# A two-layer transformer kernel: moved step places in attention, the gated state added in half precision, earlier base rows, and the row gathers in four pairs

## The chip, the cores and the metric

One core of one Trainium2 chip runs the whole program. Times are device microseconds; the time before is the median of three runs, and one further execution was taken with the hardware profiler. The engines are PE (TensorE), DVE (VectorE), ACT (ScalarE), POOL (GpSimd) and SP (SyncE, which issues DMAs).

## The reference

Two layers over x of 8 x 512 tokens, 256 wide. Each layer adds two branches of the normalised input to x.

```
xn = layernorm(x)
x  = x + attention0(xn) + moe0(xn)
xn = layernorm(x)
x  = x + gated_scan1(xn) + moe1(xn)

attention0:  16 causal heads of 16, softmax, output projection
moe0:        shared expert + 2 of 8 routed experts, silu((xW1+b1)*(xW3+b3)) W2 + b2, H = 352
gated_scan1: z = sigmoid(xWz+bz); h_t = (1-z_t) h_{t-1} + z_t (xWh+bh)_t; sigmoid(hWg+bg) * h
moe1:        latent 128, 2 of 8 experts (all computed, weighted), relu^2; shared relu^2(x up) down
```

## The kernel before, in words

**Precision.** Most products of full-precision operands are made of three half-precision products (`three_products`, lines 121 to 123): each operand is split into a high half, a half-precision copy made by ACT, and a low half, the difference, made by DVE or POOL.

**Three phases.** `mix_phase` is attention with the router of the first layer. `experts_phase` runs the first layer's experts over tiles of 256 tokens: 11 of the 16 shared tiles (head), then the routed tiles of eight experts in a hardware loop, then the last 5 shared tiles (the tail), in which the second layer's first block of 512 tokens is already prepared. `layer1_phase` runs eight steps, one for each block; step 0 and step 7 are written out, the six between are a hardware loop of two steps a turn. It has the longest code on each engine, and every engine runs its own list of instructions in order; semaphores with names such as `sc_s` (router sigmoid done) join the lists.

**Attention's order is written out by hand.** A block has 16 heads and a head three units, so a block has 48 places. At each place PE makes one unit of a head's scores transposed (`scores_k`, L854 to L858) and one unit of the next but one group's scores (`scores_q`, L839), whose row maxima DVE takes (`maxima`, L687) out of two banks in turn: PE may be two units ahead. Groups are four heads. DVE turns a group's maxima (L695) at its last place, and ACT issues four small DMAs (`load_max`, L486) that put them into the query stack, one at each of the places 0 to 3 of the group; `scores_k` of the next group waits for them. Everything else has a place of its own, given by the `AT_` constants: the next block's transposed input, q, k, v and logits; the previous block's transposed output and projection; the router; and for the block after next the statistics, the normalised rows (`normalise`, L566, two tiles at each of places 25 and 26) and `x_bias` on POOL. An operation that PE makes at a place is copied by ACT one place later, and its low half or sum is made by DVE two places later. The q and k halves are stored by SP and fetched again into the stacks (`load_stacks`, L308 to L325); the first half of the heads is needed by `scores_q` at place 24, the second at place 0 of the next block.

**The second layer's step.** PE makes the router's logits, the latent, z0, h0 (waits for `sc_s`), z1 (waits for the latent's low half), h1, eight `up` parts, the gate of the scanned state, eight experts with the `down` products between them, the next block's transposes, `combine`, then the sixteen adds of the gated state to the output banks (L2318) and the latent's last product (waits for `comb_lo_s`). ACT begins with the sigmoid L1970, then the latent's high half, the sigmoids of z, relus (L1955), squares and high halves. DVE does the router, the two injections, the scans (L2111), `sums` (L2037), low halves and the experts' squares. POOL does, in this order, the eight row gathers of the next block (`gather`, L1887: 128 rows of 1 KB each, from `y_routed`), `base` (L1894: x1 plus the shared experts' y, after `total_y` of the block before has read the buffer), four `up_low` and eight `he_lo`. The gathers wait only for the slots and for the last `sums`, so they start as soon as POOL has done the last `he_lo` of the step before. `sums(b + 1, k)` adds the weighted rows k of the next block to its base, first k = 0, later k = 1. The gated state is `gh = gs * hT` in full precision, and PE adds it by a matmul against the identity:

```
for t in range(TT):
    for c in range(DC):
        pe.matmul(out_bank[t][:, c * P:(c + 1) * P], gh[:, c, t * P:(t + 1) * P], identf[:, :],
                  start=False, stop=False)
```

**The base rows of block 0.** SP loads `xin` and `ysh` (x1 and y of the first 512 tokens) in `new_expert(E + 1)`, behind the last routed tile's store. POOL then adds them (L1325), waits for that store and issues eight gathers (L1331); DVE adds the rows in the tail's tiles 2 and 3 (`first_sums`).

## Time and profile before

| what | value |
|---|---|
| median of 3 runs | 1267.59 us (1266.76 to 1270.79) |
| the profiled execution's own time | 1274.47 us |
| its span | 1272.7 us |
| PE busy | 1134.8 us (89%) |
| DVE busy | 914.3 us (72%) |
| ACT busy | 677.0 us (53%) |
| POOL busy | 550.2 us (43%) |

Attention lasts to about 480 us of the span, the experts to 857, the second layer to the end. A step of the second layer takes 52 us and an attention block 53 to 57. A busy time is the union of an engine's instructions; a matmul's end is modelled, so PE's rows overlap, and a PE is idle only where a row has a bracket. A bracket at a row's end gives the idle time of that engine before it and what ended it; "remote" is a releaser that the trace does not name, "issue" is no wait that it shows.

### The profile page before, as it was taken

How to read it: one execution, taken by the hardware profiler on the slowest of the kernel's cores; microseconds unless marked ns; L12 is line 12 of the kernel's file. 1: busy time of each engine (PE TensorE's matmuls, PEld its weight loads, DVE VectorE, ACT ScalarE, POOL GpSimd, SP SyncE). 2: the span in 40 equal slices, each digit the busy share in tenths (PEclk: the TensorE clock that was granted, in tenths of full speed). 3: DMA queues.
4: the chain of work that ended last, by engine and by line, in shares of the span. 5: the costliest groups of instructions: out<-in, count | busy, mean ns of one | idle time of the engine just before them, and what ended most of it. 6: DMA issues, size and time to landing. Idle time of an engine off the chain costs nothing. (4 is left out here: it accounts for less than half of the span.)

```text
span 1272.7 us, 26804 instructions
## 1 busy us (share of the span) xinstructions
PE 1134.8 (89%) x8933; PEld 764.3 (60%) x8965; DVE 914.3 (72%) x2208; ACT 677.0 (53%) x1462; POOL 550.2 (43%) x758
## 2 busy tenths in 40 slices
PE   4888998888989885999999999969888998998998
PEld 2344554455455544998999898944554645545555
DVE  5678797778878835986666776748595685965965
ACT  2256565555555544666656766635364353652553
POOL 5432333323233226934444444224554735546324
PEclk9689999999999997999999999979999999999999
DMA  4337524335433204545422544424131331323203
GB/s 136 73 83 200 102 43 92 76 71 100 65 76 59 44 18 148 173 131 164 121 85 82 156 123 153 130 65 164 34 117 51 126 124 33 116 84 99 83 1 100
DMA packets 96846, 124.07 MB, mean 97 GB/s; under 512 B 14192, under 2 KB 86448, under 8 KB 95728
## 3 DMA queue, kind: packets, MB, share of 16 engines
q1 hardware_dynamic: 85744, 103.89, 30.5%
q0 software_dynamic: 6912, 18.88, 5.3%
q8 instruction: 47, 0.77, 0.3%
q10 hardware_dynamic: 4096, 0.14, 0.2%
q14 instruction: 47, 0.39, 0.1%
HBM read 83.52 MB, written 39.19 MB: 96 GB/s over the span
## 5 line engine op out<-in xcount | busy, mean ns | idle before, releaser
L476 ACT ACTIVATE p<-bank 128x384 f32<-128x384 f32 (+1 forms) x384 | 193.0, 528 | 196.1 <-PE bank L854 152.8
L687 DVE TENSOR_REDUCE neg_max<-bank 128x1 f16<-128x384 f32 (+3 forms) x352 | 218.8, 641 | 81.9 <-PE bank L842 72.5
L396 POOL TENSOR_SCALAR_AFFINE_SELECT p<-p 128x256 f32<-128x256 f32 x256 | 103.7, 410 | 260.9 <-ACT p L476 259.9
L121 PE MATMUL xbank<-gT_hi,w_hi 128*128 128x256 f16 (+1 forms) x636 | 175.6, 276 | 15.6 <-DVE gT_lo L1444 7.8
L122 PE MATMUL xbank<-gT_lo,w_hi 128*128 128x256 f16 (+1 forms) x636 | 175.5, 276 | 0.0
L123 PE MATMUL xbank<-gT_hi,w_lo 128*128 128x256 f16 (+1 forms) x636 | 175.4, 276 | 0.0
L839 PE MATMUL bank<-k_stack,q_stack 96*128 96x384 f16 (+3 forms) x512 | 134.5, 315 | 38.3 <-DVE neg_max L687 29.0
L1366 ACT ACTIVATE a<-xbank,b 128x256 f32<-128x256 f32 x159 | 74.4, 469 | 63.3 <-PE xbank L123 62.4
L1275 POOL DMA_INDIRECT fetched<-xn_dram,token_now x80 | 82.1, 1027 | 42.9 <-POOL token_now L1271 30.7
L854 PE MATMUL bank<-q_stack,k_stack 97*128 97x512 f16 (+1 forms) x256 | 91.8, 363 | 5.8 <-ACT p L476 3.3
L1451 DVE SCALAR_TENSOR_TENSOR prod<-xbank,b,a 128x256 f32<-128x256 f32 x159 | 74.0, 476 | 30.5 <-ACT a L1366 25.6
L1920 POOL TENSOR_TENSOR he_lo<-he_sq,he_hi 128x512 f16<-128x512 f32 x64 | 75.8, 1203 | 41.6 <-ACT he_hi L2006 41.6
L839 PEld LDWEIGHTS bank<-k_stack,q_stack 96*128 96x128 f16 x512 | 47.0, 100 | 77.5 <-DVE neg_max L687 54.9
L121 PE MATMUL ybank<-l_xT_hi,pack_hi 128*128 128x512 f16 x208 | 80.8, 389 | 13.1 <-ACT l_sc L1970 4.0
L121 PE MATMUL xbank<-w_hi,h_hi 128*128 128x256 f16 (+1 forms) x318 | 87.6, 275 | 1.9 <-DVE y L1466 1.9
L123 PE MATMUL xbank<-w_hi,h_lo 128*128 128x256 f16 (+1 forms) x318 | 87.5, 275 | 0.4 <-issue 0.4
L122 PE MATMUL xbank<-w_lo,h_hi 128*128 128x256 f16 (+1 forms) x318 | 87.5, 275 | 0.0
L2006 ACT ACTIVATE he_hi<-he_sq 128x512 f16<-128x512 f32 x64 | 39.4, 627 | 85.4 <-DVE he_sq L2139 85.4
L1457 DVE TENSOR_TENSOR h_lo<-h,h_hi 128x256 f16<-128x256 f32 x159 | 67.7, 429 | 22.0 <-ACT h_hi L1375 17.9
L121 PEld LDWEIGHTS xbank<-gT_hi,w_hi 128*128 128x128 f16 (+1 forms) x636 | 68.3, 107 | 24.8 <-issue 15.3
L122 PE MATMUL ybank<-l_xT_lo,pack_hi 128*128 128x512 f16 x208 | 80.6, 387 | 2.7 <-issue 2.7
L872 PE MATMUL bank<-p,v_aug 128*32 128x512 f32 (+3 forms) x1024 | 82.0, 438 | 0.8 <-DVE o_rows L667 0.8
(300 smaller groups left out, 3043.9 us busy)
## 6 DMA issues: line engine op xcount, KB each, us to landing
w_bc<-wT_dram SPq DMA_DIRECT2D x8, 2048.0 KB, 8.3
y_routed_dram<-y SPq DMA_DIRECT2D x37, 256.0 KB
w<-in_w SPq DMA_DIRECT2D x11, 704.0 KB
pack<-in_pack SPq DMA_DIRECT2D x12, 342.0 KB
xr<-in_x SPq DMA_DIRECT2D x8, 512.0 KB, 7.3
xn_dram<-xn SPq DMA_DIRECT2D x8, 512.0 KB, 3.7
qk_hi_dram<-qk_hi SPq DMA_DIRECT2D x16, 256.0 KB, 2.2
qk_lo_dram<-qk_lo SPq DMA_DIRECT2D x16, 256.0 KB, 2.2
```

The source lines that it names most:

```text
L121: pe.matmul(out, hi_a(c), hi_b(c), start=first and x == 0, stop=False)
L122: pe.matmul(out, hi_a(c), lo_b(c), start=False, stop=False)
L123: mm = pe.matmul(out, lo_a(c), hi_b(c), start=False, stop=last and x == n - 1)
L396: pool.affine_select(out=diagonal, in_=diagonal, pattern=[[0, 2], [1, P]], compare_op=ALU.is_ge, fill=0.0, base=0, channel_multiplier=-1). ...
L476: act.activation(p32[:, s // GH % 2, s % GH, cols], s_bank[n][:, 0:cols.stop - cols.start], ACT.Exp).then_inc(p_exp.sem, 1)
L687: dve.tensor_reduce(neg_max[:, g % 2, 0:GH * TT].rearrange("p (h t) -> p h t", t=TT)[:, heads[0]:heads[-1] + 1, j], a_bank[c % 2][:, 0:len ...
L839: pe.matmul(to[:, at * w:(at + 1) * w], q_stack[0:STK, u, h0 + h, j * P:(j + 1) * P], k_stack[0:STK, u, h0 + h, 0:w], start=at == 0, stop= ...
L854: mm = pe.matmul(to[:, 0:S - n * P], k_stack[0:AUG, u, h, n * P:(n + 1) * P], q_stack[0:AUG, u, h, n * P:S], start=True, stop=True)
L872: mm = pe.matmul(out_bank[VW * h:VW * (h + 1), k * P:S], v_aug[:, b % 2, k, GH * (g % NG) + h, :], p32[:, g % 2, h, P_OFF[k]:P_OFF[k] + S ...
L1275: pool.indirect_dma_start(fetched[:, u, half, :], None, dram["xn"], bass.IndirectOffsetOnAxis(token_now[:, u, half:half + 1], 0)).then_inc ...
L1366: act.activation(a1[0:M, m, :], bank[m][0:M, 0:ETOK], ACT.Identity, bias=b13[0:M, u, m:m + 1]).then_inc(a1_s.sem, 1)
L1920: pool.tensor_tensor(he_lo[:, e, :], he_sq[:, e % EB, :], he_hi[:, e, :], ALU.subtract).then_inc(he_lo_s.sem, 1)
```

## The change

Places: the transposed input goes from 0 and 2 to 1 and 3, the first q from 6 to 7, the transposed output from 13 and 16 to 14 and 17, the second projection from 24 to 25, the second v from 36 to 37; the normalised rows go from two tiles at 25 and 26 to one at each of 28 to 31, `x_bias` from 28 to 33, the router's ranks from 14 to 19 to six places up to 24; the maxima's four DMAs go out two at a place. The loads of block 0's base rows move from behind the routed tiles to the end of the head tiles. In the second layer the gathers are cut into four pairs, k = 0 first, each behind a step of ACT, with a semaphore for each k. The gated state is formed in place in `gs`, split by ACT and DVE into halves, and added by PE with a half-precision identity.

```diff
-AT_X_T, AT_Q, AT_K, AT_OUT_T, AT_PROJ, AT_V, AT_LOGITS = (0, 2), (6, 27), (9, 30), (13, 16), (21, 24), (33, 36), 39
-AT_STATS, AT_RSTD, AT_NORM, AT_XB = (21, 22), 24, (25, 26), 28
-AT_SCORES, AT_CHOICE, AT_WEIGHTS, AT_RANK_SUMS, AT_RANKS = (4, 6), (7, 8), 10, 12, (14, 15, 16, 17, 18, 19)
-AT_MAX = (0, 1, 2, 3)
+AT_X_T, AT_Q, AT_K, AT_OUT_T, AT_PROJ, AT_V, AT_LOGITS = (1, 3), (7, 27), (9, 30), (14, 17), (21, 25), (33, 37), 39
+AT_STATS, AT_RSTD, AT_NORM, AT_XB = (21, 22), 24, (28, 29, 30, 31), 33
+AT_SCORES, AT_CHOICE, AT_WEIGHTS, AT_RANK_SUMS, AT_RANKS = (4, 6), (7, 8), 10, 12, (15, 16, 18, 19, 20, 24)
+AT_MAX = {0: (0, 1), 1: (2, 3)}
...
-                        q = AT_MAX.index(at % (U * GH))
-                        load_max(group(s) - 1, range(q, q + 1))
+                        load_max(group(s) - 1, AT_MAX[at % (U * GH)])
...
-                            normalise(b + 2, halves[AT_NORM.index(at)])
+                            normalise(b + 2, range(AT_NORM.index(at), AT_NORM.index(at) + 1))
...
                 if is_int(e, E + 1):
-                    sp.wait_ge(y_stored.sem, y_stored.at(HEAD_TILES - 1))
-                    sp.dma_start(front.xin[:, :, :], token_rows(dram["x1"])).then_inc(front.xin_loaded.sem, 16)
-                    sp.dma_start(front.ysh[:, :, :], token_rows(dram["y"])).then_inc(front.xin_loaded.sem, 16)
                     return
...
             def last(e, u, first):
                 if is_int(e, 0):
                     store(HEAD_TILES - 1, dram["y"], HEAD_TILES - 1)
+                    sp.wait_ge(y_stored.sem, y_stored.at(HEAD_TILES - 1))
+                    sp.dma_start(front.xin[:, :, :], token_rows(dram["x1"])).then_inc(front.xin_loaded.sem, 16)
+                    sp.dma_start(front.ysh[:, :, :], token_rows(dram["y"])).then_inc(front.xin_loaded.sem, 16)
...
-                elif stage == 2:
+                elif stage == TAIL_TILES - 3:
                     first_sums(0)
                     first_sums(1)
-                elif stage == 3:
+                elif stage == TAIL_TILES - 2:
...
-        gathered = sig("rows_gathered", 16 * TT * 2)
+        gathered = [sig(f"rows_gathered{k}", 16 * TT) for k in range(2)]
...
-            def gather(b):
+            def gather(b, k, tiles):
...
-                for t in range(TT):
-                    for k in range(2):
-                        pool.indirect_dma_start(rows_k[:, t, k, :], None, dram["y_routed"],
-                                                bass.IndirectOffsetOnAxis(slot[:, t, k:k + 1], 0)).then_inc(gathered.sem, 16)
+                for t in tiles:
+                    pool.indirect_dma_start(rows_k[:, t, k, :], None, dram["y_routed"],
+                                            bass.IndirectOffsetOnAxis(slot[:, t, k:k + 1], 0)).then_inc(gathered[k].sem, 16)
...
             def step(b, u, before, more):
                 if more:
-                    gather(b + 1)
+                    pool.wait_ge(sc_s.sem, sc_s.at(b))
+                    gather(b + 1, 0, (0, 1))
+                    pool.wait_ge(zs_s.sem, zs_s.at(b, 1))
+                    gather(b + 1, 0, (2, 3))
+                    pool.wait_ge(zs_s.sem, zs_s.at(b))
+                    gather(b + 1, 1, (0, 1))
+                    pool.wait_ge(r_s.sem, r_s.at(b, 2))
+                    gather(b + 1, 1, (2, 3))
                     base(b + 1, 1 - u)
...
                 for c in range(DC):
                     act.wait_ge(g_psum.sem, g_psum.at(b, c + 1))
+                    act.wait_ge(gh_lo_s.sem, gh_lo_s.at(b - 1, c + 1))
...
                 if more:
                     x_high(b + 1)
+                for c in range(DC):
+                    act.wait_ge(gh_s.sem, gh_s.at(b, c + 1))
+                    act.wait_ge(out_psum.sem, out_psum.at(b - 1))
+                    act.activation(gh_hi[:, c, :], gs[:, c, :], ACT.Copy).then_inc(gh_hi_s.sem, 1)
...
-                dve.wait_ge(gathered.sem, gathered.at(b - 1, 0))
+                for k in range(2):
+                    dve.wait_ge(gathered[k].sem, gathered[k].at(b - 1, 0))
...
-                    dve.tensor_tensor(gh[:, c, :], gs[:, c, :], hT[:, c, :], ALU.mult).then_inc(gh_s.sem, 1)
+                    dve.tensor_tensor(gs[:, c, :], gs[:, c, :], hT[:, c, :], ALU.mult).then_inc(gh_s.sem, 1)
                 if more:
                     x_low(b + 1)
+                for c in range(DC):
+                    dve.wait_ge(gh_hi_s.sem, gh_hi_s.at(b, c + 1))
+                    dve.tensor_tensor(gh_lo[:, c, :], gs[:, c, :], gh_hi[:, c, :], ALU.subtract).then_inc(gh_lo_s.sem, 1)
...
-                pe.wait_ge(gh_s.sem, gh_s.at(b))
+                pe.wait_ge(gh_lo_s.sem, gh_lo_s.at(b))
                 for t in range(TT):
                     for c in range(DC):
-                        pe.matmul(out_bank[t][:, c * P:(c + 1) * P], gh[:, c, t * P:(t + 1) * P], identf[:, :],
-                                  start=False, stop=False)
+                        for gh in (gh_hi, gh_lo):
+                            pe.matmul(out_bank[t][:, c * P:(c + 1) * P], gh[:, c, t * P:(t + 1) * P], front.identh[:, :],
+                                      start=False, stop=False)
```

## Rows read from the trace of the kernel before

**Rows 1.** The page's first line

```profile
span 1272.7 us, 26804 instructions
```

**Rows 2.** Stretches: span, busy PE, PEld, DVE, ACT, POOL; granted clock, DMA share, GB/s

```profile
97.00:150.00 53.00, 47.40 (x423) 27.51 (x426) 42.91 (x113) 30.31 (x63) 18.48 (x37) 1.00 0.62 159
...
600.00:700.00 100.00, 99.58 (x912) 91.45 (x910) 66.29 (x151) 63.48 (x168) 44.28 (x62) 1.00 0.32 95
```

**Rows 3.** Waits: who waited for whom, us in total, times, longest

```profile
ACT l_sc L1970 <- remote: 47.5, 6, 7.9
```

**Rows 4.** Timeline of POOL, second layer: start, length, instruction, idle before

```profile
1017.70 0.95 POOL L1887 DMA_INDIRECT rows_k<-y_routed_dram,slot  x1 [0.30 <-issue]
...
1028.83 2.36 POOL L1894 TENSOR_TENSOR x<-xin,ysh 128x1024 f32<-128x1024 f32 x1 [10.18 <-DVE l_y L2146]
```

**Rows 5.** Timeline of ACT, the same step and, from 1223, the last

```profile
1020.40 0.20 ACT L1970 ACTIVATE l_sc<-ybank 128x32 f32<-128x32 f32 x1 [7.89 <-remote]
...
1027.18 0.60 ACT L1955 ACTIVATE r<-ybank 128x512 f32<-128x512 f32 x1 [1.41 <-PE ybank L123]
1028.39 0.60 ACT L1955 ACTIVATE r<-ybank 128x512 f32<-128x512 f32 x1 [0.61 <-PE ybank L123]
...
1223.92 0.20 ACT L1970 ACTIVATE l_sc<-ybank 128x32 f32<-128x32 f32 x1 [3.08 <-PE ybank L123]
...
1231.71 0.60 ACT L1955 ACTIVATE r<-ybank 128x512 f32<-128x512 f32 x1 [1.32 <-PE ybank L123]
```

**Rows 6.** Timelines of POOL and ACT, end of the expert stage

```profile
822.38 2.36 POOL L1325 TENSOR_TENSOR x<-xin,ysh 128x1024 f32<-128x1024 f32 x1 [20.66 <-DMA ysh<-y_dram]
...
833.75 0.95 POOL L1331 DMA_INDIRECT rows_k<-y_routed_dram,slot  x1 [0.30 <-issue]
...
836.46 0.60 ACT L1358 ACTIVATE gT_hi<-xbank 128x512 f16<-128x512 f32 x1 [5.34 <-remote]
```

**Rows 7.** Timeline of DVE, the step of rows 4

```profile
1029.63 2.65 DVE L2111 TENSOR_TENSOR_SCAN hT<-keep,inject 128x512 f32<-128x512 f32 x1
...
1032.78 1.21 DVE L2111 TENSOR_TENSOR_SCAN hT<-keep,inject 128x512 f32<-128x512 f32 x1
...
1033.91 1.64 DVE L2037 SCALAR_TENSOR_TENSOR x<-rows_k,wk,x 128x256 f32<-128x256 f32 x4
```

**Rows 8.** Timelines of PE and DVE, end of a second-layer step

```profile
1063.95 1.95 PE L2318 MATMUL ybank<-identf,gh 128*128 128x128 f32 x16
1065.73 0.27 PE L121 MATMUL ybank<-pack_hi,comb_hi 128*128 128x256 f16 x1
...
1064.78 0.69 DVE L2191 TENSOR_TENSOR comb_lo<-ybank,comb_hi 128x512 f16<-128x512 f32 x1 [4.15 <-ACT comb_hi L2012]
```

**Rows 9.** Groups of instructions, the table matmuls: busy us, mean ns, idle before

```profile
L1670 PE MATMUL xbank<-in_column,in_lane 128*128 128x114 f16 x64 | 3.5, 213 | 0.0
```

**Rows 10.** Timeline of PE in attention: places 5, 24, 29, 41 and 45 of block 1

```profile
110.83 0.34 PE L839 MATMUL bank<-k_stack,q_stack 96*128 96x384 f16 x1 [1.04 <-DVE neg_max L687]
...
131.90 0.39 PE L839 MATMUL bank<-k_stack,q_stack 96*128 96x128 f16 x4
...
139.12 0.34 PE L839 MATMUL bank<-k_stack,q_stack 96*128 96x384 f16 x1 [1.41 <-DVE neg_max L687]
...
153.06 0.34 PE L839 MATMUL bank<-k_stack,q_stack 96*128 96x384 f16 x1 [0.87 <-DVE neg_max L687]
...
157.81 0.39 PE L854 MATMUL bank<-q_stack,k_stack 97*128 97x512 f16 x1 [0.29 <-DMA q_stack<-max_rows]
```

**Rows 11.** Timeline of DVE, places 25 and 26 of the same block

```profile
135.32 0.81 DVE L566 TENSOR_SCALAR xn<-xr,mv,rstd 128x256 f32<-128x256 f32 x2
...
137.87 0.72 DVE L566 TENSOR_SCALAR xn<-xr,mv,rstd 128x256 f32<-128x256 f32 x2
```

**Rows 12.** Timeline of SP's queue, the store of k's low half

```profile
120.85 0.36 SPq L308 DMA_DIRECT2D qk_lo_dram<-qk_lo  x1
```

**Rows 13.** Groups of instructions, the routed tiles' gathers

```profile
L1275 POOL DMA_INDIRECT fetched<-xn_dram,token_now x80 | 82.1, 1027 | 42.9 <-POOL token_now L1271 30.7 <-issue 12.2
```

More of the change, by code:

```diff
@@ L1025, in __init__ @@
         self.xT_hi, self.xT_lo = (sb(f"l1_xT_{k}", [P, DC, S], F16) for k in ("hi", "lo"))
+        self.identh = sb("identh", [P, P], F16)
+        self.identh_s = sig("identh_s", 1)
         self.tile_out = sb("y", [P, ETOK // P, D])
@@ L1078, in experts_phase @@
         tail_at = sb("tail_at", [P, TAIL_PLACES])
-        identh = sb("identh", [P, P], F16)
+        identh = front.identh
         pos_part = sb("pos_part", [P, 2, T // P, 2], I32)
@@ L1118, in experts_phase @@
         lane_placed = sig("lane_placed", 1)
-        identh_s = sig("identh_s", 1)
+        identh_s = front.identh_s
         lanes_half_s = sig("lanes_half_s", 1)
@@ L1729, in layer1_phase @@
         gs = sb("gs", [P, DC, S])
-        gh = sb("gh", [P, DC, S])
+        gh_hi, gh_lo = (sb(f"gh_{k}", [P, DC, S], F16) for k in ("hi", "lo"))
         lat_hi, lat_lo = (sb(f"lat_{k}", [P, S], F16) for k in ("hi", "lo"))
@@ L1804, in layer1_phase @@
         gh_s = sig("gh_s", DC)
+        gh_hi_s = sig("gh_hi_s", DC)
+        gh_lo_s = sig("gh_lo_s", DC)
         out_psum = sig("out_psum", TT)
@@ L2032, in sums @@
                     dve.wait_ge(x2_base.sem, x2_base.at(b))
-                    dve.wait_ge(gathered.sem, gathered.at(b - 1))
+                    dve.wait_ge(gathered[0].sem, gathered[0].at(b - 1))
                 else:
+                    dve.wait_ge(gathered[1].sem, gathered[1].at(b - 1))
                     dve.wait_ge(x2_sum.sem, x2_sum.at(b, 1))
```

## The prediction

> **What bounds the kernel now.** I read the page's first line for the span, then the long waits, then the busy time by stretch, and then the timelines of the three places that the change touches. The profiled execution took 1274.5 us around a span of 1272.7 us [rows 1]. The median of the timed runs is 1267.6 us, so the profile is 6.9 us heavy. I make the sum against 1274.5 and carry it to the median by taking the same 6.9 us off. A measurement of this kernel tells about 0.3% (3.8 us) from no change.
>
> The reader should see three regimes in [rows 2]: attention (PE busy 47.40 of 53 us), the routed tiles (99.58 of 100, nothing to gain there), and the second layer, whose steps are 52 us apart. PE sets the pace of attention except where it waits, so its idle rows are the gain on offer. In the second layer one wait stands out: ACT waits before the router's sigmoid (L1970) six times, 47.5 us in all, for a releaser the profile cannot name [rows 3].
>
> **Second layer, the gathers (the largest term).** In the step before 1020.40, the last of POOL's eight back-to-back row gathers is issued at 1017.70 and done at 1018.65 [rows 4]; ACT's sigmoid starts at 1020.40, 1.75 us after that, after 7.89 us idle [rows 5]. At the end of the expert stage the same eight gathers end at 833.75 + 0.95 = 834.70, and ACT's copy that waits for PE starts at 836.46, 1.76 us after it, again "remote" [rows 6]. Two places, one distance: while a long run of gathers is under way, PE's releases reach the others late, and the last ones when the last gather has landed. The last step issues no gathers and shows the wait without them: 3.08 us [rows 5]. So a step loses 7.89 - 3.08 = 4.81 us. The change makes POOL wait for that very sigmoid before its first gather, so the hold can't fall there any more.
>
> Part comes back. During the hold PE runs ahead into the latent and z0 products; without it the first relu comes 1231.71 - 1223.92 = 7.79 us after the sigmoid in place of 1027.18 - 1020.40 = 6.78: 1.01 us back. The second piece is `base`, the add of 2.36 us on POOL (1028.83, [rows 4]), which now stands behind the fourth pair. That pair waits for the second relu. Measured from the sigmoid, this relu ends about 9.6 us on (28.39 + 0.60 - 20.40 = 8.6 in the old step, plus 1.01). Two gathers take 1.25 + 0.95 = 2.2 us (spacing and length of [rows 4]), so base runs from about 11.9 to 14.3. Before, it ran from 8.43 to 10.79, and the first scan that met it took 2.65 us where the second took 1.21 [rows 7]: DVE's scan stood still until POOL's add was over. Now the second scan meets it: it started at 1032.78, 12.38 on, and could start at 12.38 + 1.01 = 13.4, waits to 14.3 and ends at 15.4, where `sums` started at 1033.91, 13.51 on, before. From `sums` on DVE is without a pause until the experts are done, so the whole tail shifts by 1.9 us, in which the 1.01 is contained. Net per step 4.81 - 1.9 = 2.9; six steps: **17.4 us**. From below: if base costs nothing, 3.8 x 6 = 23. From above: see the second rival. Step 0 had its gathers after the products anyway; I count nothing.
>
> The Trainium skill (SBUF — State Buffer, "SBUF: two separate sides") says that a DVE operation with two SBUF inputs and a GpSimd operation that reads SBUF exclude each other for the whole instruction. The trace agrees: 2.65 against 1.21 us. It speaks against this change, because it sets base against a later scan, and without the lock the step would gain 3.8 instead of 2.9.
>
> The rest of POOL's queue behind the gathers: base, then the four up_lows, which wait for ACT's up_hi of square 4, late in the step, and keep their cover. sums(k=1) needs the fourth pair's rows only at 19.7 us after the sigmoid, the pair is issued by 12. The split of the gathered semaphore costs DVE one more wait that has long been met.
>
> **The gated state in half precision.** PE's sixteen full-precision adds take 1.78 us to the next matmul (1063.95, the next row's start being 1065.73, [rows 8]). Thirty-two half-precision ones of the same 128 columns: 64 table matmuls of 114 columns took 3.5 us, 55 ns each [rows 9], so 32 x 55 = 1.76 us. And both lie inside the wait for comb_lo, written from 1064.78 to 1065.47: even at half the price PE would go on no sooner than 1065.5. Taken: 0, bounds -0.3 and +0.5 us a step. ACT's two added copies (0.6 us each as its other copies) and DVE's two subtractions (0.69 us as comb_lo) fall between the transposed input and comb_hi, where ACT is idle for 4.4 us and DVE for 4.2. Cost 0; without that cover 1.3 us a step.
>
> **Base rows sooner.** POOL waited 20.66 us for xin and ysh, added them from 822.38 to 824.74 and then gathered [rows 6]. Now both tiles are there early, and the first gather waits only for the last routed store, which SP issues right before those two loads: some 5 us sooner, an estimate from what the loads' landing took. The 1 MB moves beside the first routed tiles, where DMA engines are a third busy (0.32, [rows 2]). But the hold (ACT idle 5.34 us before 836.46 in the same rows) moves with the gathers to the tile before, at the same price. What can go is DVE's waits for rows, which PE doesn't feel. Taken: 0.5 us; bounds -2 and +3. The two stage numbers written as TAIL_TILES minus something are the same numbers as before.
>
> **Attention places.** A place (a third of a head) is 1.1 us of PE. Take the block from 105.5 to 158.9 [rows 10]. At place 5 PE waits 1.04 us for DVE's maximum: DVE had the divide, one x_low and then another with the scores. The change moves x_low from places 2 and 4 to 3 and 5. Of 1.04 I take 0.9. At place 29 it waits 1.41 us, because DVE ran divide, residual and four normalised tiles through places 25 and 26 (the tiles alone 0.81 and 0.72, [rows 11]). The change puts the residual at 27 and a tile each at 28 to 31. I take 1.2. At place 41 it waits 0.87 (v_bias, now at 39), and at place 45 0.29 for the maxima's DMA, now issued two places sooner. But those rows queue beside the stacks' loads, and a PE that is early there only waits longer: I take 0.4 of 1.16. Between places 12 and 24 I take nothing: PE starts on the next block's stacks at 131.90 without a wait, and their arrival is set by a chain of DMAs that begins when k's low half is stored, after place 11 (120.85, [rows 12]): store, its landing, six loads of 128 KB. Whatever PE saves before place 24 it waits there. Sum 2.5 us a block, six full blocks, 1 us for the first and last: **16 us**. Bounds: 0.5 a block (the new places only move the waits: the transposed output's low half is now a place later, with the projection at 21 waiting for it) and 4 a block. The moved x_bias on POOL (2.4 us, place 28 to 33) delays no mask that a value product waits for; its DVE neighbours change, its length doesn't.
>
> **Sum.** 17.4 + 0 + 0.5 + 16 = 33.9: 1274.5 becomes 1240.6 profiled, 1267.6 becomes 1233.7; I say 1234.
>
> **The rivals.**
> *Only the gathers help* (0.12): the attention waits move to the stacks' and maxima's DMAs. For it: no wait at 131.90. Against it: places 29 and 5 are plain DVE backlog. 1267.6 - 17.9 = 1250, within 1.
> *The hold follows the gathers* (0.15): each run of gathers delays PE's releases wherever it stands, and now it stands where ACT, DVE and PE hand over every 1.3 us. Against it: the routed stage issues 80 gathers two at a time [rows 13] and its PE is 99.6% busy. For it: three of the four pairs follow nearly at once. If 2.5 of the 2.9 us go, 1267.6 - 16.5 - 2.4 = 1249.
> *Neither helps* (0.05): 1265.
> *Slower* (0.06): each pair holds releases until its own landing, 2.2 + 1.75 = 3.95 us, and three of the four pairs have someone waiting: 11.9 us held plus 1.9 for base against 4.81 saved is +9.0 a step, +54 in all, less 16.5: 1305. It decides against the change as soon as the holds pass about 5.6 us a step (2.9 + 16.5 / 6).
> *The forecast* (0.62).
>
> The range runs from 1217 (3.8 a step, 4 a block) to 1256 (half of either term and a dearer base). Faster by more than 0.3%: 0.89; within: 0.05; slower: 0.06.
>
> **What would show it.** ACT's idle before L1970 near 3 us and never "remote"; steps 49 us apart in place of 52; base starting 12 us after the sigmoid with a long second scan; PE's wait for neg_max below half; the wait at place 24 put down to the k_stack load; L2318 with 256 matmuls and no wait for gh_lo. It is wrong if "remote" waits appear before the relus or zs, or if attention's span stays within 3 us of before.

## The result: 0.992 of the time before, a quarter of the forecast gain

The changed kernel takes 1259.73 us (median of seven runs, 1254.64 to 1265.4) against 1268.36 (1266.76 to 1271.89) for the kernel before, a ratio of 0.9921 with a 95% interval of 0.9904 to 0.9939. The forecast was 1234, with a range from 1217 to 1256. The gain is 8.6 us where 33.6 were expected.

The profiled execution of the changed kernel took 1258.37 us, about its median. That of the kernel before took 1274.47, heavier than all seven of its timed runs, so the two profiles differ by 16.1 us, of which 6.1 are the older profile's excess over its median and 1.4 are what the newer one lies below its own.

Of the page, kernel after, the first line and the group of the second layer's gathers (busy us, mean ns, idle before and what ended most of it); POOL now stands 63.3 us waiting for the sigmoid, which is what the change asks of it:

```profile
span 1256.6 us, 26994 instructions
...
L1889 POOL DMA_INDIRECT rows_k<-y_routed_dram,slot x56 | 61.9, 1105 | 91.9 <-ACT l_sc L1979 63.3
```

Where the 16.1 us are is read from two landmarks that both kernels have: the copy of the identity at the start of the expert stage, and the eight router sigmoids of the second layer. The tile view of each kernel (first the kernel before, then the one after: count, durations in ns, first and last start):

```profile
L1413 ACT ACTIVATE identh<-identf x1: 309/309/309, 481.9 to 481.9; 128x128 f16<-128x128 f32 x1
...
L1970 ACT ACTIVATE l_sc<-ybank x8: 197/198/198, 862.1 to 1223.9; 128x32 f32<-128x32 f32 x8
```

```profile
L1414 ACT ACTIVATE identh<-identf x1: 309/309/309, 463.2 to 463.2; 128x128 f16<-128x128 f32 x1
...
L1979 ACT ACTIVATE l_sc<-ybank x8: 197/197/198, 845.0 to 1208.1; 128x32 f32<-128x32 f32 x8
...
  PE ybank L123: 20.2, 7
```

Attention ends 18.7 us sooner. The experts take 381.8 us in place of 380.2. The seven steps between the first and the last sigmoid take 363.1 us in place of 361.8: **the second layer, where 17.4 us were expected, gives nothing**. And yet the wait of [rows 3] is gone: seven sigmoids now idle 20.2 us together, 2.9 each, and none is put down to "remote". The hold went, and something of the same size came.

The timeline of DVE, POOL and ACT in one step (its sigmoid at 1055.31; four of the seven steps are like it) shows what, beside [rows 4, 5, 7]:

```profile
1055.31 0.20 ACT L1979 ACTIVATE l_sc<-ybank 128x32 f32<-128x32 f32 x1 [2.89 <-PE ybank L123]
...
1065.63 1.21 DVE L2127 TENSOR_TENSOR_SCAN hT<-keep,inject 128x512 f32<-128x512 f32 x1
...
1065.78 1.81 POOL L1889 DMA_INDIRECT rows_k<-y_routed_dram,slot  x1 [1.59 <-issue]
...
1067.90 0.95 POOL L1889 DMA_INDIRECT rows_k<-y_routed_dram,slot  x1 [0.30 <-issue]
...
1068.22 4.10 DVE L2127 TENSOR_TENSOR_SCAN hT<-keep,inject 128x512 f32<-128x512 f32 x1
...
1068.87 2.35 POOL L1896 TENSOR_TENSOR x<-xin,ysh 128x1024 f32<-128x1024 f32 x1
...
1072.24 1.64 DVE L2053 SCALAR_TENSOR_TENSOR x<-rows_k,wk,x 128x256 f32<-128x256 f32 x4
```

The first gather of the fourth pair meets the first scan and takes 1.81 us where the next takes 0.95. The second scan begins while the last gather is under way and ends at 1072.3, 1.1 us after POOL's add is over: it stood through the gather and the add that follows it without a pause. The sums start 16.93 us after the sigmoid; in the step of [rows 5, 7] it was 13.51.

The other three steps (sigmoids at 845.01, 898.00 and 1001.64) lose the time in another way. No scan is long in them: both gathers of the fourth pair meet a scan, the add starts 14.1 to 15.1 us after the sigmoid, and the sums wait for it until 16.6 to 17.6. Timelines of POOL and DVE in the step from 1001.64:

```profile
1015.04 1.70 POOL L1889 DMA_INDIRECT rows_k<-y_routed_dram,slot  x1 [0.30 <-issue]
...
1016.76 2.36 POOL L1896 TENSOR_TENSOR x<-xin,ysh 128x1024 f32<-128x1024 f32 x1
...
1019.25 2.57 DVE L2053 SCALAR_TENSOR_TENSOR x<-rows_k,wk,x 128x256 f32<-128x256 f32 x4 [3.26 <-POOL x L1896]
```

PE, which waits for the scanned state's high half, shows the price twice. The timeline of PE, step from 1055.31:

```profile
1072.18 0.38 PE L123 MATMUL ybank<-l_xT_hi,pack_lo 128*128 128x512 f16 x1
1075.75 0.39 PE L121 MATMUL ybank<-hT_hi,pack_hi 128*128 128x512 f16 x1 [3.19 <-DVE up_sq L2132]
...
1077.62 0.63 PE L122 MATMUL ybank<-hT_lo,pack_hi 128*128 128x512 f16 x1
1078.05 0.63 PE L123 MATMUL ybank<-hT_hi,pack_lo 128*128 128x512 f16 x1
```

It idles 3.19 us, and then the matmuls, 0.21 us apart before, are 0.43 us apart: the granted clock has fallen to half, 1.2 GHz. A stretch of this step and one of the step from 1001.64, in which PE idled 4.71 us, until 1023.68 (columns as in [rows 2]; the rest of both steps has 1.00):

```profile
1076.90:1080.30 3.40, 3.40 (x10) 1.22 (x9) 3.40 (x4) 1.64 (x4) 3.40 (x3) 0.50 0.88 295
```

```profile
1022.30:1029.10 6.80, 5.42 (x13) 1.94 (x14) 5.67 (x11) 2.35 (x4) 2.56 (x2) 0.50 0.97 309
```

3.4 us at half clock cost 1.7 us. Four of the seven steps have 3.4 us of it, two (from 845.01 and 1001.64) have 6.8, the last has none: 27.3 us in all, of which PE was idle for 2.3, so 12.5 us are lost, where the kernel before loses 1.7. Over the seven the granted clock is 0.96, where it was 0.99 before. The first row is before, the second after:

```profile
862.10:1223.90 361.80, 327.97 (x2076) 189.26 (x2076) 265.93 (x598) 172.76 (x322) 183.65 (x171) 0.99 0.27 89
```

```profile
845.00:1208.10 363.10, 325.37 (x2076) 187.97 (x2076) 272.87 (x612) 182.71 (x336) 197.25 (x175) 0.96 0.28 88
```

In attention PE's wait for the row maxima falls from 27.2 to 10.1 us (waits of PE from 51 to 480 us, before and after):

```profile
PE bank L839 <- DVE neg_max L687: 27.2, 42, 1.5
```

```profile
PE bank L838 <- DVE neg_max L686: 10.1, 29, 1.4
```

### The profile page after: what moved, and what is told of

It is laid out like the page before. It is cut to its first block and busy times, and to the rows that moved or that the text cites. A ratio compares the mean times of both kernels' runs of the same rounds, so it can differ in the third digit from the quotient of the medians.

```text
span 1256.6 us, 26994 instructions
## 1 busy us (share of the span) xinstructions
PE 1133.0 (90%) x8964; PEld 756.0 (60%) x8965; DVE 921.3 (73%) x2224; ACT 683.9 (54%) x1478; POOL 559.2 (45%) x758
## 5 line engine op out<-in xcount | busy, mean ns | idle before, releaser
L1889 POOL DMA_INDIRECT rows_k<-y_routed_dram,slot x56 | 61.9, 1105 | 91.9 <-ACT l_sc L1979 63.3
L1929 POOL TENSOR_TENSOR he_lo<-he_sq,he_hi 128x512 f16<-128x512 f32 x64 | 77.1, 1223 | 32.2 <-ACT he_hi L2016 32.2
L841 PE MATMUL bank<-mask_qk,identb 128*128 128x128 bf16 (+2 forms) x352 | 88.6, 252 | 0.0
```

Of the source, the lines that this page charges most:

```text
L841: pe.matmul(diagonal, identb[:, :], mask_qk[:, 0:len(heads), :], start=False, stop=True).then_inc(a_psum.sem, 1)
L1929: pool.tensor_tensor(he_lo[:, e, :], he_sq[:, e % EB, :], he_hi[:, e, :], ALU.subtract).then_inc(he_lo_s.sem, 1)
```

## The experiments

Sixteen runs stand in four groups, each group on one chip with its own runs of the kernel before: 1270.27, 1245.72, 1245.05 and 1271.15 us. I call the first and the last chip A and D, the others B and C. Between groups only ratios and the lengths of stages are compared.

**Which stage, which part (chip A).** One: the kernel before again, unchanged.

> The kernel before, unchanged, profiled once more, because its profiled execution (1274.47 us) lies above all seven of its timed runs (1266.76 to 1271.89). If the two profiles differ by a stage, the router's sigmoids of the second layer or the start of the expert stage stand elsewhere than at 862.06 to 1223.92 and 481.92 us. Theory 1 (the excess is chance, spread over the stages): attention ends within 2 us of 482, the seven intervals between sigmoids sum to 362 within 2 us. Theory 2 (the change's gain in attention is partly an unlucky execution of before): attention ends 4 to 7 us sooner here. In both the held sigmoids are there: six waits of 7.9 us.

1269.86 us. Attention ends at 477.5 in place of 481.9, the seven steps take 361.7 us (857.7 to 1219.4), and the sigmoids are held as before:

```profile
L1413 ACT ACTIVATE identh<-identf x1: 309/309/309, 477.5 to 477.5; 128x128 f16<-128x128 f32 x1
...
L1970 ACT ACTIVATE l_sc<-ybank x8: 197/197/198, 857.7 to 1219.4; 128x32 f32<-128x32 f32 x8
...
  remote: 47.7, 6
```

So theory 2: of the 4.6 us between the two profiled executions 4.4 lie in attention. Against this execution attention's gain is 14.3 us, not 18.7. It is one execution, and whether its chip is that of the first profile isn't known.

Two: the places alone (`AT_` constants, `load_max`, `normalise`; the rest as before).

> Before, with the new places of attention alone. Theory 1 (the profile's 18.7 us between the two kernels in attention are this part's): 1268 - 17 = 1251, within 3, and the second layer as before with six held sigmoids near 7.9 us. Theory 2 (only part of it is real, the rest chance of one execution): 1256 to 1260.

1257.04 us, 0.9883 (0.9856 to 0.9910): 13.2 us less. Attention ends at 463.2 as in the changed kernel, the second layer is the old one (361.5 us, six held sigmoids, 47.5 us). The stage saves the 14 that the second profile of before says: theory 2.

Three: all but the places.

> The changed kernel with the places of attention as before; gathers in pairs, half-precision gated state and the sooner base rows stay. Theory 1 (in the second layer what the sigmoid no longer waits, the second scan waits behind POOL's last pair and its add of the base rows): 1268 within 3, the intervals between sigmoids 51 to 52 us, the second scan about 4.1 us long. Forecast of the record: 1250. Theory 2 (a loss that the attention places hide): above 1272.

1280.05 us, 1.0066 (1.0043 to 1.0090): **the other three parts together make the kernel slower by 9.8 us**, where the forecast had 17.9 faster. The steps take 373.7 us, 52.4 to 54.3 each, and neither theory names the cause. It isn't the scan that stands still here (none takes over 1.22 us) but POOL: both gathers of the fourth pair meet a scan (1.81 and 1.70 us), the add starts only 15.2 us after the sigmoid, and the sums wait for it until 17.7 (the step from 959.6; the others are alike). PE then waits 4.6 to 4.8 us, and 6.8 us are at half clock in five of the seven steps, 3.4 in two, 41 us in all. The code has the pair wait for the second relu of ACT, and that relu was released late, after the third pair of gathers (timeline of ACT; at this place it idles 0.70 us in the changed kernel's step from 1055.31, and 1.3 to 1.7 in that kernel's three steps without a long scan):

```profile
969.49 0.60 ACT L1965 ACTIVATE r<-ybank 128x512 f32<-128x512 f32 x1 [1.54 <-PE ybank L123]
```

Four: the add moved.

```diff
                     gather(b + 1, 0, (2, 3))
+                    base(b + 1, 1 - u)
                     pool.wait_ge(zs_s.sem, zs_s.at(b))
                     gather(b + 1, 1, (0, 1))
                     pool.wait_ge(r_s.sem, r_s.at(b, 2))
                     gather(b + 1, 1, (2, 3))
-                    base(b + 1, 1 - u)
```

> The changed kernel with POOL's add of the base rows (2.35 us) moved ahead of the third pair of gathers, so that it lies from about 6.3 to 8.7 us after the sigmoid, between the two scans' inputs and the first scan at 10.3. Theory 1 (the second scan waits for the base add, which POOL begins in the same moment as the last gather lets go): the second scan falls from 4.1 us to 1.2 or 1.9, the sums start near 14.3 us after the sigmoid in place of 16.9, seven steps each lose 2.6: 1260 - 18 = 1242, within 4. Theory 2 (PE's releases are held behind each pair of gathers, wherever the add is): the step stays at 51 us and the time at 1260, within 3.

1250.01 us, 0.9831 (0.9806 to 0.9857): 20.3 us less than before, between the two theories. The second scan takes 1.21 us and the first sums start 14.04 us after the sigmoid, as theory 1 has it. But the add waits for DVE's `total_y` until 8.66 us after the sigmoid, so the last gathers are late, and the second sums wait 5.13 us for their rows; PE then waits 2.61 and again runs 3.4 us at half clock (timelines of POOL, DVE and PE in the step from 995.7, then a stretch):

```profile
1012.15 1.28 POOL L1889 DMA_INDIRECT rows_k<-y_routed_dram,slot  x1 [0.30 <-issue]
...
1021.12 1.67 DVE L2053 SCALAR_TENSOR_TENSOR x<-rows_k,wk,x 128x256 f32<-128x256 f32 x4 [5.13 <-DMA rows_k<-y_routed_dram,slot]
...
1024.65 0.39 PE L121 MATMUL ybank<-lat_hi,pack_hi 128*128 128x512 f16 x1 [2.61 <-DVE he_sq L2155]
```

```profile
1025.00:1028.40 3.40, 3.40 (x16) 2.01 (x14) 3.30 (x8) 1.47 (x3) 2.31 (x2) 0.50 0.02 5
```

Step 0, where the last gather was done at 14.0 and no sum waited, took 48.0 us, the others 51.

Why those rows are late can be read from the trace, though no run tested it. The last gather starts at 1012.15, and at 1012.65 SP issues the load of `w_bc`, 2 MB, and by 1014.42 three more of 512 KB. The DMA engines are then nearly full until the rows are there, where in the 4 us before their busy share was 0.29 (timeline of SP, then a stretch):

```profile
1012.65 0.35 SPq L1871 DMA_DIRECT2D w_bc<-wT_dram  x1
```

```profile
1012.70:1020.70 8.00, 7.70 (x49) 4.47 (x48) 3.15 (x5) 5.04 (x10) 5.84 (x5) 1.00 0.92 299
```

In step 0 the last gather was done 2.5 us before this load was issued, and its rows came in time.

**The next order, and the small parts (chip B).** Five: the add between the third and the fourth pair.

```diff
                     gather(b + 1, 1, (0, 1))
+                    base(b + 1, 1 - u)
                     pool.wait_ge(r_s.sem, r_s.at(b, 2))
                     gather(b + 1, 1, (2, 3))
-                    base(b + 1, 1 - u)
```

> The changed kernel with POOL's add of the base rows between the third and the fourth pair of gathers. In the kernel that has it before the third pair, the second scan is cured but the last gather is done only at 17.7 us after the sigmoid, its rows arrive at 24.95 and the second sums start at 25.4 in place of 20.4, whereas its step 0, with the last gather done at 14.0, needs 47.96 us. Theory 1 (a step is 48 us when neither a scan nor the second sums wait): pair three stays at 6.7 to 8.9, the add runs from 8.9 to 11.3 with the first scan behind it (done near 12.4 in place of 11.5), pair four is done near 13.5, the second sums start by 21: six to seven steps of 48 to 48.5 us, the granted clock near 1.00 in them, 1260 - 7 x 3 = 1239, within 4. Theory 2 (the gathers hold PE's releases wherever they are, so a step with eight of them can't be under 51 us): 1256 to 1262.

1228.01 us, 0.9865 (0.9843 to 0.9888). The steps are 47.2 to 49.1 us, and no clock is lost in them: theory 1 for the steps. But the ratio is no better than attention's alone, because this chip's kernel before takes 1245.72, and the next three say why.

Six: one run of eight gathers behind the sigmoid, then the add.

> The changed kernel with the eight gathers in one run directly behind the sigmoid, without ACT's steps between the pairs, then the add of the base rows. Theory 1 (a long run of gathers holds PE's releases until its end, as before the sigmoid in the kernel before): the run goes from 1.1 to 11.1 us, the latent's copy, the zs and the relus late by 4 to 5 us, the step 53 us or more, 1270 or above. Theory 2 (nothing is held: the idle time before the sigmoid had another cause; only the exclusion with DVE's scans costs): the run ends at 11.1, the add at 13.5, the first scan waits a gather, the second about 1.2 us, and the step is under 50: 1248 or less.

1235.33 us, 0.9911 (0.9887 to 0.9935), steps of 48.4 to 49.8. The relus start 7.8 to 7.9 us after the sigmoid (6.55 in step 0), in the middle of the run, as with no gathers: nothing is held here, theory 2 on this chip.

Seven and eight: one small part each.

> The kernel before with the half-precision gated state alone. The record said 0, between -0.3 and +0.5 us a step, because both forms end inside PE's wait for comb_lo; if the cover were missing it would be 1.3 us a step. Theory 1: 1270, within 3 us, PE's wait before the combine's products longer by what the products save. Theory 2 (the shorter products do come through, since the copies on ACT and the subtractions on DVE take the time between the input's low half and comb_hi): 1262 to 1266. Theory 3 (the added operations push comb_hi and so the next sigmoid): 1275 or more.

> The kernel before with the two loads of the first base rows issued one expert sooner, nothing else. The record said 0.5 us less, between -2 and +3 saved. Theory 1: 1270, within 3 us; POOL's wait for the rows shorter by 5 us or more, ACT's hold in the last routed tiles at another tile but as long. Theory 2 (the hold goes with the run of gathers into a tile where PE has slack): up to 5 us less, 1265.

1244.23 us, 0.9985 (0.9971 to 1.0000), and 1245.21 us, 1.0000 (0.9981 to 1.0019): theory 1 of both, with 1.5 us, if anything, for the first. Both have the gathers of the kernel before, in one run that passes over the sigmoid, and no sigmoid is held (tile view of the eighth kernel, then its seven steps as a stretch):

```profile
L1970 ACT ACTIVATE l_sc<-ybank x8: 197/198/198, 854.5 to 1193.3; 128x32 f32<-128x32 f32 x8
...
  PE ybank L123: 21.6, 7
```

```profile
854.50:1193.30 338.80, 321.29 (x2075) 189.74 (x2076) 264.02 (x598) 173.94 (x323) 182.59 (x172) 1.00 0.30 95
```

**The hold on which the largest term rested comes and goes with the chip.** These steps take 361.7 us on chip A and 338.8 here with the same code of the second layer: 22.9 us, where the medians of the kernel before are 24.6 apart. The experts are 4.8 us shorter here as well, attention 1.6 longer. Each chip was used in one group of runs only, so a property of the chip and a state that it was in can't be told apart.

**All on one chip without a hold (chip C).** Nine to twelve: the changed kernel, the gathers alone, everything but the gathers, and the fifth kernel again.

> The changed kernel unchanged, beside the three that follow, on one chip. So far one chip gave 1270 us for the kernel before, with the held sigmoids in its profile, and another 1246, where the same order of gathers has steps of 48 to 49 us and no held sigmoid. Theory 1 (the hold is a property of the chip, and the pair order costs what it costs on either): on the chip of 1270 it is 0.992 of before as recorded; on the chip of 1246 the second layer gets slower than before by 2 to 3 us a step (the scan behind the add), and only attention's 14 us stand against it: 1246 - 14 + 7 x 2.6 = 1250, a ratio of 1.00. Theory 2 (the hold goes with the kernel, not with the chip): a ratio of 0.992 on both.

> The kernel before with the gathers in four pairs and the add behind them alone. Theory 1: on the chip of 1270, 1280 as with the half-precision state and the sooner base rows beside it (1.007); on the chip of 1246, no hold to remove, so the full price of the late add shows: 1246 + 18 = 1264, a ratio near 1.015. The record's term (17.4 us less) would be 0.986. Theory 2 (the price came from the half-precision state's added waits beside the gathers): 1.00 or less.

> The changed kernel with the gathers and the add as before. Theory 1: attention's gain alone, and nothing from the other two: 0.988 of before on either chip, and on the chip of 1246 the fastest of the four or level with the next. Theory 2 (the parts need each other): over 0.995.

> The changed kernel with the add between the third and the fourth pair, once more, to stand beside the other three on one chip. Theory 1: on the chip of 1246 again 0.9865, level with the kernel that has the gathers as before, since there is no hold there to gain from; on the chip of 1270 steps of 48 to 49 us in place of 51 to 52, so 1240 or a ratio of 0.977. Theory 2 (on the chip of 1270 the gathers late in the step arrive late, as the fourth pair did at 24.95 us after the sigmoid): 51 us a step, 0.985.

| kernel | median us | ratio (95%) | seven steps, us |
|---|---|---|---|
| the kernel before | 1245.05 | | |
| changed kernel | 1241.92 | 0.9972 (0.9956 to 0.9988) | 353.3 |
| gathers alone | 1259.53 | 1.0104 (1.0080 to 1.0128) | 357.3 |
| all but the gathers | 1225.78 | 0.9847 (0.9825 to 0.9869) | 337.3 |
| add before the last pair | 1229.05 | 0.9867 (0.9846 to 0.9888) | 339.6 |

Theory 1 is the nearer one throughout, though three of its numbers were too high: the changed kernel came to 1242 where it had 1250, the gathers alone to 1259.5 for 1264, all but the gathers to 0.985 for 0.988. That last kernel saves 19.3 us here, where the places alone saved 13.2 on chip A and the two small parts 1.5 and 0 on chip B; no run shows where the other 4 to 5 us come from. Where nothing is held the four pairs with the add behind them cost 14.5 us alone, 16 in the changed kernel (1241.92 against 1225.78). Two of its seven steps have the long scan that four had in the first profile. In the other five the second scan starts at the same place and takes 1.21 us, and it is the add that is long: it takes 2.7 us in place of 2.35, and the sums wait 2.3 us for it (a step of each kind: scan, then add):

```profile
1002.46 1.22 DVE L2127 TENSOR_TENSOR_SCAN hT<-keep,inject 128x512 f32<-128x512 f32 x1
...
1003.12 2.72 POOL L1896 TENSOR_TENSOR x<-xin,ysh 128x1024 f32<-128x1024 f32 x1
```

```profile
1052.85 4.11 DVE L2127 TENSOR_TENSOR_SCAN hT<-keep,inject 128x512 f32<-128x512 f32 x1
...
1053.51 2.35 POOL L1896 TENSOR_TENSOR x<-xin,ysh 128x1024 f32<-128x1024 f32 x1
```

Both kinds make PE pause 2.7 to 3.2 us behind them, and the clock goes with it in six of the seven steps (seven steps of the changed kernel, then of the one without the gathers' change):

```profile
839.40:1192.70 353.30, 322.58 (x2076) 187.66 (x2077) 270.09 (x612) 183.54 (x338) 197.39 (x175) 0.97 0.28 91
```

```profile
838.30:1175.60 337.30, 316.02 (x2076) 183.13 (x2076) 273.40 (x612) 181.13 (x338) 182.65 (x171) 1.00 0.29 95
```

**A chip that holds again (chip D).** Thirteen and fourteen: the two best of chip C.

> The changed kernel with the gathers and the add as before, on another call's chip. Theory 1 (attention's gain on any chip): 0.985 to 0.988 of before. On a chip that holds: six sigmoids idle 7.9 us, 1270 x 0.988 = 1255. On one that doesn't: 1226.

> The changed kernel with the add between the third and fourth pair. Theory 1 (the hold is the chip's and needs gathers before the sigmoid): on a chip that holds, steps of 48.5 to 49 us, 1240, a ratio of 0.977, and ahead of the gathers as before (1255) by 12 to 15; on one that doesn't, 1229, behind them by 3. Theory 2 (such a chip holds the releases behind the pairs too): 51 us a step, 0.987, level with them.

1259.36 us, 0.9907 (0.9882 to 0.9933), with six sigmoids waiting 48.2 us for "remote"; and **1232.50 us, 0.9715 (0.9691 to 0.9740)**, with none. Theory 1 of both in kind, not in size: the first lies above its 0.985 to 0.988 (three of its steps lose 1.7 us each to the clock), the second is 7.5 us better than its 1240. With the add before the last pair the clock stays up on this chip too. After step 0 the scans run freely here, where on chips B and C the first of them takes 2.05 us, and the first sums start 14.3 us after the sigmoid in most steps (seven steps as a stretch, then POOL and DVE in the step from 986.1):

```profile
839.60:1181.90 342.30, 316.81 (x2075) 182.74 (x2076) 268.11 (x612) 179.30 (x336) 195.56 (x175) 1.00 0.29 94
```

```profile
995.00 2.38 POOL L1896 TENSOR_TENSOR x<-xin,ysh 128x1024 f32<-128x1024 f32 x1
...
997.31 1.22 DVE L2127 TENSOR_TENSOR_SCAN hT<-keep,inject 128x512 f32<-128x512 f32 x1
...
999.32 1.22 DVE L2127 TENSOR_TENSOR_SCAN hT<-keep,inject 128x512 f32<-128x512 f32 x1
...
999.61 1.68 POOL L1889 DMA_INDIRECT rows_k<-y_routed_dram,slot  x1 [0.30 <-issue]
...
1000.45 1.65 DVE L2053 SCALAR_TENSOR_TENSOR x<-rows_k,wk,x 128x256 f32<-128x256 f32 x4
```

This version beats the kernel before on all three chips where it ran, and the changed one beside it on chip C by 12.9 us; where nothing is held, leaving the gathers as before is 3 us better still.

Fifteen and sixteen: one group of places each.

```diff
-AT_X_T, AT_Q, ... = (0, 2), (6, 27), ...
+AT_X_T, AT_Q, ... = (1, 3), (7, 27), ...
```

> The kernel before with only the transposed rows' places moved (0 and 2 to 1 and 3, the first q product from 6 to 7). The record gave 0.9 us a block for it, PE's wait of 1.04 us at place 5: 0.9 x 7 = 6 us less. Theory 1: 0.995, the wait at place 5 at 0.25 us or under. Theory 2 (it only moves the wait to a place nearby, because the next q product waits for the low half): 1.000.

```diff
-AT_STATS, AT_RSTD, AT_NORM, AT_XB = (21, 22), 24, (25, 26), 28
+AT_STATS, AT_RSTD, AT_NORM, AT_XB = (21, 22), 24, (28, 29, 30, 31), 33
...
-                            normalise(b + 2, halves[AT_NORM.index(at)])
+                            normalise(b + 2, range(AT_NORM.index(at), AT_NORM.index(at) + 1))
```

> The kernel before with only the four normalised tiles and x_bias moved (25, 26 and 28 to 28 to 31 and 33). The record gave 1.2 us a block for PE's wait of 1.41 us at place 29: 8.4 us less. Theory 1: 0.993, no wait at place 29. Theory 2 (the divides and the residual that stand at 24 to 26 make the wait without the tiles): 0.998 to 1.000.

1267.92 us, 0.9981 (0.9971 to 0.9992), 3.2 us less; and 1263.54 us, 0.9942 (0.9924 to 0.9961), 7.6 us less. The first lies between its theories: PE's wait at place 5 goes from 1.04 to 0.44 us, not to 0.25. The second is theory 1. PE's waits in block 1: of the fifteenth kernel those at places 5 and 29 (the one at 41 is 0.88); of the changed one all over 0.2 us. The sixteenth has none at 29, and 0.87 us at 41 as before.

```profile
107.54 0.34 PE L839 MATMUL bank<-k_stack,q_stack 96*128 96x384 f16 x1 [0.44 <-DVE neg_max L687]
...
135.98 0.34 PE L839 MATMUL bank<-k_stack,q_stack 96*128 96x384 f16 x1 [1.42 <-DVE neg_max L687]
```

```profile
107.82 0.34 PE L838 MATMUL bank<-k_stack,q_stack 96*128 96x384 f16 x1 [0.25 <-DVE neg_max L686]
...
117.62 0.66 PE L881 MATMUL bank<-identf,o_cols 128*128 128x128 f32 x4 [0.38 <-ACT o_cols L491]
...
120.97 0.34 PE L838 MATMUL bank<-k_stack,q_stack 96*128 96x384 f16 x1 [0.27 <-DVE neg_max L686]
...
148.35 0.34 PE L838 MATMUL bank<-k_stack,q_stack 96*128 96x384 f16 x1 [0.28 <-DVE neg_max L686]
```

## Why the prediction was wrong

**Second layer, the gathers: 17.4 us forecast, 9.8 us lost with its two small companions on chip A, 14.5 lost alone on chip C.** This is the step that failed. Its parts:

- *The hold goes.* 4.81 us a step: right, on a chip that has it. All sigmoids idle 2.9 us in the changed kernel.
- *"base runs from about 11.9 to 14.3 ... the second scan ... waits to 14.3 and ends at 15.4."* The mechanism was named and under-sized. Measured on the same scale, in the step from 1055.31, the add runs from 13.56 to 15.91 and the scan ends at 17.0. The pair before it takes 3.07 us, not 2.2: I had let only the add exclude the scans, and the gathers do too (1.81 against 0.95 us). The rest is POOL's start: the relu ends 9.68 us after the sigmoid and the gather starts at 10.47, where I let it start at 9.6. So 3.42 us come back between this step and that of [rows 7], not 1.9. The steps of the kernel before alternate (13.51 and 13.07 to the first sums, 14.45 in step 0), and three of the changed kernel's are of the other kind; each taken against its own, it is 2.1 to 4.1 us, 25.3 over the seven.
- *"Six steps", "Step 0 ... I count nothing."* Seven steps pay, step 0 too, and only six had a hold.
- *The clock* was in no term: 3.4 or 6.8 us at half clock behind PE's pause in six steps, 12.5 us lost against 1.7 before.

Together, as an estimate from these rows, 6 x 4.81 = 28.9 saved against 25.3 + 10.8 = 36.1 lost, less what PE no longer waits elsewhere (0.6 us before the next block's transposes in six steps, 1.33 to 0.74, and 0.2 a step in the gated state, 4.9 in all): about +2.3. The profiles differ by +1.3 us, where -17.4 stood. My bound from below, 23 us "if base costs nothing", was the step in which nothing collides, and the fifth kernel comes near it on chip D (342.3 us for the seven steps, 362.5 in the fifteenth kernel, which has the gathers as before, 20.2 us apart). The bound on the other side was missing: no gather was let collide with a scan of 1.21 us [rows 7], seven steps were six, and the term was never let fall below zero, so the range ended at 1256.

The exclusion is a rule that the forecast cited, and it was right to weigh it: the Trainium skill (SBUF — State Buffer, "SBUF: two separate sides") has whichever of the two starts first keep the port for its whole instruction. The runs agree in part. A scan that starts during the last gather takes 4.10 us where one with no neighbour takes 1.21, and between the gather and the add, 0.02 us apart, it isn't let in. But in five steps of the changed kernel on chip C, and in one with the gathers alone, the scan starts at the same place in the same gather (12.9 us after the sigmoid, the gather at 12.6; in step 0 both 1.2 us sooner) and takes 1.21 us, and the add takes 2.7: either of the two can lose, and what decides it isn't known. Both times the sums are late, at 16.9 and at 16.4 us. The Trainium skill (SBUF — State Buffer, "SBUF: two separate sides") also says that POOL can't write the descriptors of a DMA it issues while DVE runs an operation in a 2-port perf mode; of one with two SBUF inputs it doesn't say so. The first gather of the fourth pair, beside a scan, took 1.8 us in place of 0.95 in every one of the seven steps, and the forecast had no price for it.

**Attention: 16 us forecast, 13.2 measured alone (14.3 in the stage).** Right within its bounds. The normalised tiles: 1.2 us a block forecast, 8.4 in seven; 7.6 measured. The transposed rows: 0.9 a block; 3.2 in all, about 0.5 a block, since the wait fell only to 0.44 us. Place 41: 0.4 us forecast with place 45, and 0.87 has become 0.28. *"Between places 12 and 24 I take nothing"* erred a little too: the waits of 0.48 and 0.40 us that stand there in the sixteenth kernel are gone in the changed one, and one of 0.27 has come.

**Half precision: 0 forecast, 1.5 us measured (0.9985, hardly apart from none).** That is inside the bound of -0.3 us a step. But *"sixteen full-precision adds"* was a misreading: the loop issues eight adds a step, which make sixteen rows (128 in the eight steps), so the change issues sixteen products, not thirty-two. From the first of them (1102.71) to the next product, PE's wait for comb_lo included, it is 1.58 us in place of 1.78 [rows 8]:

```profile
1104.29 0.28 PE L121 MATMUL ybank<-pack_hi,comb_hi 128*128 128x256 f16 x1 [0.52 <-DVE comb_lo L2210]
```

**Base rows: 0.5 forecast, nothing measurable (1.0000).** The hold moved to a tile before at about the same price, as said (4.50 us, changed kernel; [rows 6] had 5.34). But ACT goes on at 806.92 here, while the eighth gather runs only from 807.88: that a hold lasts until the last gather has landed, as the forecast read it from two places, doesn't hold at this one:

```profile
806.92 0.47 ACT L1367 ACTIVATE a<-xbank,b 128x256 f32<-128x256 f32 x1 [4.50 <-remote]
```

**The rivals.** "Slower: each pair holds releases" had the sign right for this part and the wrong mechanism. "The hold follows the gathers" is true in a small way on chips that hold: 0.6 to 1.0 us at one relu in the three steps without a long scan. The changed kernel's seven steps take 363.1 us there and 353.3 on chip C, where that relu is never late; how much of that difference is this relu's wasn't measured apart. The time came near "only the gathers help" turned round: only attention helps.

**Open.** What makes PE's releases late under gathers on two chips (and where the first profiles were taken) and not on two others isn't known; no run took it apart. Rows of a gather done at 17.7 us arrive only at 24.95 in the fourth kernel, on chip A; that they queue beside the 2 MB load is the trace's reading (with the add before the last pair that gather is done by 15.2 and no sum waits), and no run moved the load.

## What to carry to other kernels

When POOL's work is moved, lay its instructions, gathers included, over DVE's two-input operations one by one, and count a collision as the whole run of POOL instructions that follow each other without a pause, not as the one it meets first. Look at every step, not at one: here seven steps of the same code lost their time in two ways. Count the clock with a pause: in nearly all of these steps 2.6 to 3.2 us of waiting were followed by 3.4 us at half clock, which makes it half as dear again. And a wait that the trace can't name may come with the chip and not with the kernel: before a term rests on it, see it on a second chip.

## What the runs showed that was not expected

The kernel before takes 1270 us on two chips and 1245 on two others. Most of the difference is in seven steps of the second layer, in which ACT waits 7.9 us for a release of PE while POOL issues gathers on the one kind and 2.9 to 3.1 on the other. So one and the same edit is worth different things: the changed kernel's ratio is 0.9921 where it was first measured, where the sigmoids are held, and 0.9972 on chip C; the fifth kernel's is 0.9715 on chip D and 0.9867 on chip C.
